# Setup of a six-block Perceiver kernel: query weights first on SyncE's queue, latents behind them in eight transfers, bias rows on ScalarE's queue

## The reference, cut to what matters

```python
def _layernorm(x, axis=-1, eps=1e-05):
    m = jnp.mean(x, axis=axis, keepdims=True)
    v = jnp.var(x, axis=axis, keepdims=True)
    return (x - m) / jnp.sqrt(v + eps)

x = x + cross_attention(ctx_1024, _layernorm(x), mask, g1, b1, g2, b2, Wq, Wkv, Wout)  # 16 heads of 64
x = x + gated_linear_recurrence(_layernorm(x), ...)
x = x + ffn(_layernorm(x), ...)        # weights rounded to 4 bits in blocks of 32
x = x + cross_attention(_layernorm(x), ctx_1024, ...)
x = x + self_attention(_layernorm(x), ...)
x = x + mixture_of_experts(_layernorm(x), ...)
```

## Time and profile before

| | |
|---|---|
| median of 3 runs | 2055.35 us (2054.4 to 2057.96) |
| the profiled execution | 2053.8 us |
| its span in the profile | 2051.7 us |
| share of the span, PE / DVE / ACT / POOL | 84% / 78% / 73% / 44% |
| setup, up to its barrier | about 39 us |

### The profile page before, as it was taken

One profiled execution on the slowest core, in us unless ns is written; L12 is line 12 of the kernel. 1 busy time (PEld: TensorE's weight loads), 2 busy tenths in 40 slices (PEclk: granted clock), 3 DMA queues, 4 the chain that ended last, 5 costly groups with the idle time before them and its releaser, 6 DMA issues. The chain is left out here.

```text
span 2051.7 us, 51500 instructions
## 1 busy us (share of the span) xinstructions
PE 1718.3 (84%) x13455; PEld 1392.9 (68%) x13455; DVE 1594.6 (78%) x4998; ACT 1504.4 (73%) x4156; POOL 908.9 (44%) x1339
## 2 busy tenths in 40 slices
PE   3599999999999999971710679999999799749997
PEld 3489999999999999941500356666667566427775
DVE  4798888888888888837788669999999588636664
ACT  3488888888888888854765479999999588545553
POOL 1544444444444444304156034444444377335554
PEclk8599999999999999995755799999999799879998
DMA  4277676777777777610000059999999300103322
GB/s 139 85 167 165 160 160 157 161 163 162 159 162 163 159 160 164 151 42 0 0 0 0 2 147 250 252 250 251 249 249 248 73 1 0 32 13 102 91 87 82
DMA packets 196234, 259.54 MB, mean 127 GB/s; under 512 B 25136, under 2 KB 141328, under 8 KB 196032
## 3 DMA queue, kind: packets, MB, share of 16 engines
q1 hardware_dynamic: 194678, 256.53, 50.0%
q10 hardware_dynamic: 1194, 1.58, 0.3%
q0 software_dynamic: 288, 0.56, 0.1%
HBM read 86.09 MB, written 4.72 MB: 44 GB/s over the span
## 5 line engine op out<-in xcount | busy, mean ns | idle before, releaser
L778 ACT ACTIVATE a_prob<-a_neg,a_nmax 128x289 f32<-128x289 f32 x512 | 266.6, 525 | 1.4 <-DVE a_nmax L705 1.1
L840 PE MATMUL a_out<-a_probT,a_xn 128*128 128x256 f32 x1024 | 263.0, 380 | 5.0 <-DMA a_probT<-a_blocks 4.2
L1710 ACT ACTIVATE b_prob<-b_neg,b_nmax 128x257 f32<-128x257 f32 x512 | 260.6, 515 | 6.9 <-DVE b_nmax L1661 6.8
L671 POOL TENSOR_TENSOR a_xn<-a_z,g 128x256 f32<-128x256 f32 x128 | 93.8, 733 | 384.6 <-DVE a_z L739 384.6
L830 PE MATMUL a_score<-a_xnT,a_qT 128*128 128x290 f32 x1536 | 252.9, 314 | 2.5 <-DVE a_qT L750 2.5
L705 DVE CUSTOM_DVE_ANT_0 a_neg<-a_score,a_bias 128x289 f32<-128x289 f32 x512 | 211.6, 458 | 41.2 <-PE a_score L830 36.8
L786 ACT ACTIVATE a_prob<-a_prob,a_rinv 128x289 f32<-128x289 f32 x512 | 231.3, 527 | 1.8 <-DVE a_rinv L755 1.7
L830 PEld LDWEIGHTS a_score<-a_xnT,a_qT 128*128 128x128 f32 x1536 | 222.3, 190 | 9.6 <-issue 3.3
L1661 DVE CUSTOM_DVE_ANT_0 b_neg<-b_score,b_bias 128x257 f32<-128x257 f32 x512 | 188.6, 419 | 30.5 <-PE b_score L1801 15.3
L840 PEld LDWEIGHTS a_out<-a_probT,a_xn 128*128 128x128 f32 x1024 | 175.2, 191 | 19.8 <-DMA a_probT<-a_blocks 5.3
L716 DVE STREAM_TRANSPOSE a_blocks<-a_prob 128x1024 f32<-128x1024 f32 x128 | 159.4, 1245 | 24.0 <-ACT a_prob L786 17.7
(11 more groups left out here) (478 smaller groups left out, 4567.9 us busy)
## 6 DMA issues: line engine op xcount, KB each, us to landing
a_probT<-a_blocks SPq DMA_DIRECT2D x512, 192.0 KB, 3.6
b_probT<-b_blocks SPq DMA_DIRECT2D x256, 256.0 KB, 4.6
a_raw<-in_ctx SPq DMA_DIRECT2D x128, 128.0 KB, 2.9
b_raw<-in_ctx SPq DMA_DIRECT2D x64, 256.0 KB, 4.7
m_wide<-expert_weights SPq DMA_DIRECT2D x128, 128.0 KB, 2.9
a_kept<-keep SPq DMA_DIRECT2D x32, 257.0 KB, 3.4
b_kept<-keep SPq DMA_DIRECT2D x32, 257.0 KB, 4.8
b_v_rows<-ctx_tail_values SPq DMA_DIRECT2D x32, 256.0 KB, 4.7
```

The lines of the kernel that those rows point to most:

```text
L778: nc.scalar.activation(prob[:, par, grp, 0:KEYS0], neg[:, grp, :], ACT.Exp, bias=nmax[:, par, grp:grp + 1], scale=-1.0, accum_out=rsum[:, ...
L840: nc.tensor.matmul(out_ps[:, half, 0:2 * P], xn[:, j, kt, :], probT[:, u, 2 * half:2 * half + 2, kt, :], start=(kt == 0), stop=False)
L1710: nc.scalar.activation(prob[:, (j + 5) % 4, grp, :], neg[:, par, grp, :], ACT.Exp, bias=nmax[:, par, grp:grp + 1], scale=-1.0, accum_out=r ...
```

## The change

`x` is no longer one transfer of 2 MB but eight of 256 KB, each with a semaphore of its own, and they stand behind `wq` on SP's queue. The five bias rows that SP issued are issued by ACT. DVE's loop over the statistics is written out, and waits for one transfer ahead of each four tiles. Nothing else is changed, and no arithmetic.

```diff
-        first_loaded, loaded, pool_loaded, x_loaded = ..., k.sem("x_loaded")
+        first_loaded, loaded, pool_loaded, x_loaded = ..., [k.sem(f"x_loaded{c}") for c in range(CHUNKS)]
...
             @block.sync
             def _(sp):
-                sp.dma_start(k.x[:].rearrange("p (t d) -> p t d", d=D),
-                             io["x"].rearrange("(t b) l d -> (b l) t d", b=BPT)).then_inc(x_loaded, 16)
-                for dst, src in first[1::2]:
+                for dst, src in first[1:2]:
                     sp.dma_start(dst, src).then_inc(first_loaded, 16)
+                for c in range(CHUNKS):
+                    sp.dma_start(k.x[:, c * CH:(c + 1) * CH].rearrange("p (t d) -> p t d", d=D),
+                                 io["x"][c * 16:(c + 1) * 16].rearrange("(t b) l d -> (b l) t d", b=BPT)).then_inc(x_loaded[c], 16)
                 for dst, src in by_sync:
                     sp.dma_start(dst, src).then_inc(loaded, 16)
...
             @block.vector
             def _(dve):
-                dve.wait_ge(x_loaded, 16)
-                with dve.Fori(0, TILES // 4) as g:
+                for c in range(CHUNKS):
+                    dve.wait_ge(x_loaded[c], 16)
                     for j in range(4):
-                        last = tile_stats(k, g * 4 + j)
+                        last = tile_stats(k, c * 4 + j)
                     last.then_inc(stats_ready, 1)
...
             @block.scalar
             def _(act):
-                for dst, src in first[0::2]:
+                for dst, src in first[0:1] + first[2:]:
                     act.dma_start(dst, src).then_inc(first_loaded, 16)
```

More of the change, by code:

```diff
@@ L237, in setup @@
         ps = [stack.enter_context(nc.psum_tensor(f"setup_ps{j}", [P, CH], F32)) for j in range(4)]
-        first_loaded, loaded, pool_loaded, x_loaded = k.sem("first_weights_loaded"), k.sem("weights_loaded"), k.sem("weights_loaded_pool"), k.sem("x_loaded")
+        first_loaded, loaded, pool_loaded, x_loaded = k.sem("first_weights_loaded"), k.sem("weights_loaded"), k.sem("weights_loaded_pool"), [k.sem(f"x_loaded{c}") for c in range(CHUNKS)]
         ident_ready, consts_ready = k.sem("ident_ready"), k.sem("consts_ready")
```

## The result

The changed kernel takes 2133.87 us (median of 4 runs, 2132.5 to 2138.02), the kernel before 2056.65 us beside it: a ratio of 1.0379 (95% interval 1.036 to 1.0399), 77 us slower. The forecast was 2054.6, no change. The profiled execution, 2138.02 us, is the slowest of the four, so the two traces lie further apart than the medians: 84.4 us by the span.

A forecast was written before the change was run, and what follows sets the result against it. Setup was taken as bound by SP's issues of 27 loads, then DVE, PE and ACT work; 0 + 0 - 0.7 + 0 on the 2055.35 us median gave 2054.6, range 2052.1 to 2057.3, low end drawn out to 2051.0.

The forecast's parts named there:

- part 1: DVE's statistics in setup, chunk by chunk: the loop's pause of 0.22 us a turn goes, covered by the load wait; 0 us.
- Rival 3: Behind setup: PE's low-clock stretches shift against the work, about 1.2 us, either sign; chance 0.07, half each way beyond 4 us.
- 0.83 for no change: Whole kernel: chance given to a time that cannot be told from before, within about 0.2%, 4.1 us.
- Part 2: `wq` ahead of `x` on SP's queue: `x` delayed 1.0 us (0.5 to 1.7), landing about 18.3; stall ends at 13.9.
- Part 3: Eight transfers for `x`, five rows off SP's queue: SP's loads move by -0.95 or -0.54 us, taken as -0.7.
- Part 4: Ten rows on ACT's queue: PE starts 1 to 3 us earlier, at 16 to 18, lengthening its wait; 0 us.
- Rivals 1 and 2: Setup: SP not stuck, 3.6 to 5 us faster, chance 0.14; or each part of `x` pays its completion, 2067.3 us, 0.05.
- Rival 2: Setup's transfers of `x`: parts do not overlap, seven gaps of 1.8 us, 12.6 us in all; 2067.3 us, chance 0.05.

## Why the prediction was wrong

The step that failed is part 1: "The loop's pause of 0.22 us a turn goes" and "Value: 0 us". It priced the written-out loop by what it does in setup, and there it was right: DVE's statistics ended at 19.62 and left it idle 11.43 us for the loads (forecast: near 19.5, some 10). It did not ask what the added instructions do to code that stands behind. The runs showed 75 us for that, 5.8 us for each of the 13 jumps back; in the trace it is 6.1 us. Of these, 4.9 are DVE's two pauses. The rest goes with PE's clock, at 0.96 instead of 1.00, and with engines that wait for each other once more; the two were not told apart. Rival 3 had the right place, "what lies behind", and the wrong mechanism and size. The 0.83 for no change took in nothing of it.

The other parts, by their own terms (their sum was -0.7 us, and setup ended 2.0 us later):

- **Part 2.** The delay was taken as 1.0 us, between 0.5 and 1.7. With `wq` first and nothing else, the stall ends 1.4 us later, but all of `x` is there only at 19.28 instead of 17.34, so 1.9 us later; with the whole new order and the loop kept it is 19.62. Mis-sized, and for the landing outside the range. It cost nothing, since DVE waits for the loads in any case.
- **Part 3.** The stall ended at 13.90 in the last part of `x` and held `head_of_feature` until 15.03 (forecast 13.9 for one of the two), and `fenwick` started at 15.08, 0.2 us later than before instead of 0.5 to 1 earlier. "The parts of `x` are the same packets" was false. The rows for the earlier trace rows, 5 to 13 us:

```profile
q1 hardware_dynamic: 1737, 1.06, 46.7%
q10 hardware_dynamic: 1120, 0.86, 36.2%
```

  That is 1737 packets for 1.06 MB where it was 629 for 1.29: the eight transfers went in smaller packets (the trace has 1624 of 512 bytes among these). What that did to the shares is seen against the run with `wq` first, which has the same order and `x` in one transfer:

```profile
q1 hardware_dynamic: 592, 1.30, 51.6%
...
q10 hardware_dynamic: 583, 0.67, 25.4%
```

  ACT's queue got more beside the small packets (the rows alone had left it at 23.9%). So `wout` and the rows came sooner, and PE started at 14.50, before the forecast 16 to 18. That the stall's end came out near the forecast is in part luck: 13.90 us was right although the packets behind it were not those of the account.
- One term was missing: `b`'s issue, the last but one, took 1.66 instead of 0.43 us. In all three profiles with the eight transfers and 27 loads on SP one late issue is stretched so, at 26 to 28 us, when PE comes to the end of its products. It stands beside a single packet on a second instruction queue, q8 (26 to 28 us of the changed kernel; the packet starts at 26.57):

```profile
q8 instruction: 1, 0.02, 3.3%
```

  In the other two it starts at 26.86 and 26.54. In every other run, PE being later or SP done sooner, it comes at least 3.3 us after the start of `bproj`'s issue, and no load that SP issues behind the stall takes over 0.5 us. That q8 fetches PE's code, and that the fetch holds up SP's issue, is likely by this timing and was not tried. With the later start the longer issue brings `bproj` to 28.06 instead of 25.9.
- **Part 4.** 0 us, right: PE's early start went into idling. But the idling cost something after all. PE's clock was granted 0.50 from 31 to 39 us, where it was 0.92 before, after PE had idled 3.94 us:

```profile
31.00:39.00 8.00, 4.84 (x21) 3.85 (x22) 6.84 (x17) 3.48 (x17) 0.00 (x0) 0.50 0.06 16
```

  From the start of `fg` to the end of `f_downT` took 2.71 us (40.69 - 37.98) instead of 1.88. Of the 2.0 us by which setup is later, the loads are 1.17 (31.04 - 29.87) and this 0.83.
- Rivals 1 and 2 did not happen: SP was stuck as before, and the parts overlapped. The fit of 2 us for each DMA that Rival 2 names stands in the Trainium skill, DMA: Bandwidth & Descriptors, section "Anatomy of one DMA — SWDGE (gpsimd) path", and is one for transfers that GpSimd issues, which these are not.

## What to carry to other kernels

Before pricing an edit by what it does in its own place, count how many instructions it adds to each engine's program, and look for loops behind it that are longer than one block (here 256). A loop of 275 was exposed, and by the count above in some 18 of every 256 places. By the same count a longer loop would have more bad places; none was tried. The number of instructions that ran hides this: the page has 51500 before and 51425 after, though the program became longer. In a trace the signs are idle time "by issue" at a loop's start in every turn and packets on an instruction queue in the steady part of a loop; and idle instructions added ahead of the loop, more of them than there are bad places (24 here), settle the matter in one run.

## What the runs showed of the hardware that I had not expected

- A loop of 275 instructions on DVE costs nothing in some places (0, 8, 32 instructions added) and about 6 us a turn in others (12, 16, 24), 3.7% of this kernel.
- A load of 2 MB into rows of 16 KB went in packets of 2 KB (1.29 MB in 629), the same bytes in eight loads in smaller ones. The other queue's share rose from 25.4% to 36.2% from 5 to 13 us.
- One issue of SP took 1.4 to 1.8 us instead of 0.43 in the three runs in which an instruction packet of 16 KB moved at the same time.
- PE, which began earlier and then idled 3.94 us for the loads, ran its last groups of setup at a granted clock of 0.50 (1.2 GHz).
